# Index stage of a graph network kernel: statistics and roots in pairs of tiles, the running count summed in PSUM

## The chip, the cores and the metric

The kernel runs on one core of a Trainium2 chip. The metric is the device time of one execution in microseconds (us); the median of three runs is compared. TensorE is PE in the rows, VectorE DVE, ScalarE ACT, GpSimd POOL, SyncE SP. "Row sums" below are TensorE's matmuls with a column of ones.

## The reference

A graph block of four residual parts on 10000 nodes of 512 features and 5000 edges: graph convolutions, experts, attention over the edges, and a top-two mixture. Only the start of the first part matters here:

```python
    x = x + _L0_gnn_ref(_layernorm(x, axis=-1), src, dst, ...)
    # in _L0_gnn_ref:
        out_deg = jnp.clip(jax.ops.segment_sum(ones, src, num_segments=N), 1.0)
        in_deg = jnp.clip(jax.ops.segment_sum(ones, dst, num_segments=N), 1.0)
        src_norm = (out_deg ** (-0.5))[:, None]
        dst_norm = (in_deg ** (-0.5))[:, None]
        for i in range(n_layers):
            mu = jnp.mean(x, axis=0)
            var = jnp.var(x, axis=0)
    ...
```

The index stage computes two things at once: for every edge its rank among the edges sorted by source and by target, with both degrees (a counting sort that writes edge records in sorted order to memory), and the sum and the sum of squares of each column of the row-normalized x.

## The kernel before

`index_and_stats` is the first large stage of the program; later stages read what it leaves. The edges stand in 40 columns of 128 (ET = 40), the nodes in 79 tiles of 128 rows (NT = 79; the last has 16 rows). A key is split into a high part (one of NH = 80) and a low part (one of 128); `is_hi` and `is_lo` are its one-hot forms.

Each engine has its own list of instructions, written by hand; semaphores order them. A loop over t, the edge loop, runs through the 40 columns, and two node tiles go along with each turn of it (`reached`). The twelve first tiles (AHEAD) are worked ahead of the loop.

- **Node tiles.** SP loads a tile into a ring of twelve (R). DVE (`stats`, by `layer_norm`) takes the tile's row statistics, aggregates them and adds EPS, three instructions, each waiting for the one before. POOL (`root`) raises the variance to the power -1/2 and forms the shift. ACT (`norm_and_square`) normalizes the tile and squares it. TensorE (`add_up`) adds both up over the rows into psN and psQ, four passes of 512 columns a tile. In turn t, DVE and POOL handle tiles 12+2t and 13+2t, ACT tiles 10+2t and 11+2t, TensorE tiles 8+2t and 9+2t (LAG = 4).
- **Edges.** `seen` is the running count: for each key, where the next edge with it goes. Per turn, TensorE turns the one-hot low parts (`turn`) and counts the column's keys (`histogram`, into psH); DVE adds that count to `seen`; ACT casts `seen` to bf16 (`cast_seen`) and the turned picks (`spread`); DVE forms the rest that the cast lost (`lower`); TensorE looks the counts up from both parts (line 402); DVE takes for each edge its own value out (lines 500 to 510). Every fourth turn DVE writes places and degrees for four columns; POOL then grades them (`grade`, again a power) and scatters two records per column to memory (`scatter`).
- **Order.** In turn t, ACT casts the count of turn t+1 first, then spreads, then normalizes the turn's two tiles. TensorE makes the histogram of turn t+1 at the start of turn t, ahead of the row sums, and looks up after them. POOL's turn is two roots, the grading if it is due, two scatters.

Before the loop, TensorE counts all keys (psL), DVE scans, and TensorE makes the first offsets (lines 385 and 387), which DVE copies to `seen` (line 460).

Of the kernel before, what the change touches and what calls it, by code (L numbers as in the profile page):

```python
# [183 lines left out]
def index_and_stats(nc, g, x, src, dst, attr, total, square):  # L184
# [6 lines left out]
    assert FULL * ET == E and NT <= 2 * ET + AHEAD and ET % G == 0 and 5 * NH <= 512 and EP < 1 << 15  # L191
    with Phase(nc, "index") as ph:
# [9 lines left out]
        seen = ph.sb("seen", [P, 2, 2, NH])  # L202
# [21 lines left out]
        mv = ph.sb("mv", [P, R, 3])  # L224
# [43 lines left out]
        def _(act):  # L268
            def norm_and_square(n):
                r, j, k = node_rows(g, n), n % R, n % S  # L270
                act.wait_ge(rooted, 2 * n + 2)
# [13 lines left out]
            def cast_seen(t):  # L285
                act.wait_ge(counted, t + 1)
# [18 lines left out]
        def _(pool):  # L305
            def root(n):
                r, j = node_rows(g, n), n % R
                pool.wait_ge(stat_step, 3 * n + 3)
                if n >= R:
                    pool.wait_ge(normed, n - R + 1)  # L310
                pool.sem_inc(waited, 1)
                pool.tensor_tensor(rstd[0:r, j:j + 1], mv[0:r, j, 2:3], g.minus_half[0:r, 0:1], ALU.pow).then_inc(rooted, 1)
                pool.wait_ge(rooted, 2 * n + 1)
# [21 lines left out]
            for n in range(AHEAD):  # L335
                root(n)
            for t in range(ET):
                for n in reached(t, 0):
                    root(n)
# [10 lines left out]
        def _(pe):  # L350
# [32 lines left out]
            histogram(0)  # L383
            pe.wait_ge(scanned, 1)
            pe.matmul(psL[:, 1, 0:2 * NH], g.before[:, :], whole[:, :, :].rearrange("l n h -> l (n h)"),
                      start=True, stop=False)
            pe.matmul(psL[:, 1, 0:2 * NH], g.ones[:, :], upto[:, :, :].rearrange("l n h -> l (n h)"),
                      start=False, stop=True).then_inc(based, 1)
# [20 lines left out]
        def _(v):  # L409
            chain = Chain(v, stat_step, 3)  # L410

            def stats(n):
                r, j = node_rows(g, n), n % R
                v.wait_ge(loaded[j], 16 * (n // R + 1))
                if n >= R:
                    v.wait_ge(rooted, 2 * (n - R) + 2)
                chain.at(n)
                layer_norm(v, chain, xt[0:r, j, :], st[:, j, :], mv[:, j, :], r, waited)
                chain.end()
# [15 lines left out]
            for n in range(2):  # L435
# [5 lines left out]
                for stat in range(n * AHEAD // 2, (n + 1) * AHEAD // 2):  # L441
                    stats(stat)
# [17 lines left out]
            v.tensor_copy(seen[:, 0, :, :].rearrange("l n h -> l (n h)"), psL[:, 1, 0:2 * NH]).then_inc(counted, 1)  # L460
            v.wait_ge(counted, 1)
            step(v.tensor_scalar(nodes[:, :, :], seen[:, 0, :, :], -ZERO, None, ALU.add))
# [10 lines left out]
            def lower(t):  # L473
# [3 lines left out]
                v.tensor_tensor(tabs[:, t % 2, 1, 2:5:2, :], seen[:, t % 2, :, :], tabs[:, t % 2, 0, 2:5:2, :],  # L477
# [4 lines left out]
            for t in range(ET):  # L482
                j = t % 2
                if t + 1 < ET:
                    v.wait_ge(histed, t + 1)
                    v.wait_ge(counted, t + 1)
                    if t >= 1:
                        v.wait_ge(lowered, t)
                        v.wait_ge(cast, t)
# [1883 lines left out]
```

## Time and profile before

| | us |
|---|---|
| median of 3 runs | 3903.74 (3902.39 to 3907.45) |
| the profiled execution | 3906.87 |
| its span, first to last instruction | 3905.1 |
| TensorE busy in the span | 3254.1 (83%) |
| DVE busy | 2462.7 (63%) |
| ACT busy | 1388.0 (36%) |
| POOL busy | 1235.2 (32%) |

1.8 us of the profiled execution lie outside its span, and it stands 3.1 us above the median. The shares are means over many stages. The index stage fills the first 280 us of the span, and its edge loop runs from about 56 to 254 us. Busy time counts an operation from its start to its end, so that operations back to back overlap a little. Two ends of one stage are of interest: DVE's last result of the loop, and POOL's last scatter, after which the stage waits for the scattered records to land.

### The profile page before, as it was taken

The numbers are of one execution on the slowest core, as the hardware profiler recorded it, in microseconds if no ns is written. First come the engines' busy times: TensorE is split into PE (matmuls) and PEld (weight loads), VectorE is DVE, ScalarE is ACT, GpSimd is POOL, SyncE is SP. The second block draws the span as 40 slices with busy tenths as digits, with TensorE's granted clock in tenths as the row PEclk, the third lists the DMA queues.
The fourth block names the chain that finished last, engine by engine and source line by source line (L and its number), as shares of the span: only waits on it lengthen the run. The fifth ranks groups of instructions, "written<-read, shape, count | busy, mean of one in ns | idle before, by whom it ended". The sixth has DMA issues, their size and how long they took to land. (4 is left out here: it accounts for less than half of the span.)

```text
span 3905.1 us, 61914 instructions
## 1 busy us (share of the span) xinstructions
PE 3254.1 (83%) x18334; PEld 2750.4 (70%) x18335; DVE 2462.7 (63%) x5844; ACT 1388.0 (36%) x2580; POOL 1235.2 (32%) x1606
## 2 busy tenths in 40 slices
PE   6845889997775309999999999999679992969999
PEld 1213667776774209999999999999668881856766
DVE  7855877644766764545455444454278877957776
ACT  4633655421112314445444444444211111114443
POOL 4752532222551012323222322323123320025552
PEclk9977999997555559999999999999889995989999
DMA  4313323335994034544444444444322111146663
GB/s 157 99 24 105 106 94 122 100 124 167 305 306 135 0 76 113 133 116 136 126 111 137 102 133 143 99 137 113 66 64 59 54 43 42 67 122 149 161 155 104
DMA packets 250361, 449.60 MB, mean 115 GB/s; under 512 B 65632, under 2 KB 71073, under 8 KB 249591
## 3 DMA queue, kind: packets, MB, share of 16 engines
q1 hardware_dynamic: 176425, 280.66, 22.0%
q0 software_dynamic: 62368, 145.38, 17.1%
q10 hardware_dynamic: 11318, 20.54, 1.4%
q8 instruction: 119, 1.95, 0.2%
q14 instruction: 131, 1.07, 0.1%
HBM read 319.38 MB, written 126.83 MB: 114 GB/s over the span
## 5 line engine op out<-in xcount | busy, mean ns | idle before, releaser
L1460 PE MATMUL experts_psU<-experts_x_hi,experts_up_hi 128*128 128x312 f32 (+1 forms) x1408 | 443.3, 315 | 22.9 <-issue 16.5
L1489 PE MATMUL experts_psY<-experts_hid_hi,experts_dn_hi 128*128 128x312 f32 (+1 forms) x1408 | 439.0, 312 | 0.0
L1461 PE MATMUL experts_psU<-experts_x_lo,experts_up_hi 128*128 128x312 f32 (+1 forms) x1408 | 436.8, 310 | 0.0
L1462 PE MATMUL experts_psU<-experts_x_hi,experts_up_lo 128*128 128x312 f32 (+1 forms) x1408 | 435.6, 309 | 0.0
L1490 PE MATMUL experts_psY<-experts_hid_lo,experts_dn_hi 128*128 128x312 f32 (+1 forms) x1408 | 431.3, 306 | 0.0
L1491 PE MATMUL experts_psY<-experts_hid_hi,experts_dn_lo 128*128 128x312 f32 (+1 forms) x1408 | 429.7, 305 | 0.0
L1419 POOL DMA_INDIRECT experts_xg<-xn,experts_token_i x96 | 123.4, 1285 | 663.0 <-DVE experts_token_i L1586 643.5
L1625 DVE TENSOR_TENSOR experts_hid_lo<-experts_hid,experts_hid_hi 128x312 fp32r<-128x312 f32 (+1 forms) x352 | 161.2, 480 | 252.2 <-ACT experts_hid L1552 252.2
L1550 ACT ACTIVATE experts_hid_hi<-experts_psU,experts_bup 128x312 fp32r<-128x312 f32 (+1 forms) x352 | 183.6, 522 | 322.1 <-PE experts_psU L1462 320.3
L1460 PEld LDWEIGHTS experts_psU<-experts_x_hi,experts_up_hi 128*128 128x128 f32 (+1 forms) x1408 | 265.2, 188 | 24.4 <-issue 22.0
L1617 DVE TENSOR_TENSOR experts_dn_lo<-experts_dn_raw,experts_dn_hi 128x1536 fp32r<-128x1536 f32 (+1 forms) x128 | 208.0, 1625 | 98.6 <-ACT experts_dn_hi L1528 98.4
L1461 PEld LDWEIGHTS experts_psU<-experts_x_lo,experts_up_hi 128*128 128x128 f32 (+1 forms) x1408 | 265.6, 189 | 0.0
L1490 PEld LDWEIGHTS experts_psY<-experts_hid_lo,experts_dn_hi 128*128 128x128 f32 (+1 forms) x1408 | 265.5, 189 | 0.0
L1462 PEld LDWEIGHTS experts_psU<-experts_x_hi,experts_up_lo 128*128 128x128 f32 (+1 forms) x1408 | 265.4, 188 | 0.0
L1491 PEld LDWEIGHTS experts_psY<-experts_hid_hi,experts_dn_lo 128*128 128x128 f32 (+1 forms) x1408 | 265.3, 188 | 0.0
L1489 PEld LDWEIGHTS experts_psY<-experts_hid_hi,experts_dn_hi 128*128 128x128 f32 (+1 forms) x1408 | 264.9, 188 | 0.0
L772 PE MATMUL gcn_psZ<-gcn_wa_hi,gcn_agg_hi 128*128 128x512 f32 x480 | 200.8, 418 | 7.5 <-DVE gcn_diff L900 7.5
L1612 DVE TENSOR_TENSOR experts_x_lo<-experts_psT,experts_x_hi 128x416 fp32r<-128x416 f32 x96 | 56.7, 590 | 232.8 <-ACT experts_x_hi L1523 232.8
L1528 ACT CAST experts_dn_hi<-experts_dn_raw 128x1536 fp32r<-128x1536 f32 (+1 forms) x128 | 175.8, 1374 | 57.1 <-PE experts_psY L1491 45.3
L1722 PE MATMUL score_psP<-score_w_hi,score_x_hi 128*128 128x512 f32 x480 | 193.8, 404 | 0.0
L1430 POOL DMA_INDIRECT x<-experts_y,experts_token_i x96 | 157.8, 1644 | 111.6 <-DVE experts_y L1604 84.1
L1723 PE MATMUL score_psP<-score_w_lo,score_x_hi 128*128 128x512 f32 x480 | 190.1, 396 | 0.0
(412 smaller groups left out, 8158.7 us busy)
## 6 DMA issues: line engine op xcount, KB each, us to landing
experts_dn_raw<-in_L_ffn_W_down SPq DMA_DIRECT2D x96, 768.0 KB, 4.6
conv<-gcn_diff SPq DMA_DIRECT2D x120, 256.0 KB, 2.9
experts_up_raw<-in_L_ffn_W_up SPq DMA_DIRECT2D x32, 682.5 KB, 8.4
index_xt<-in_x SPq DMA_DIRECT2D x78, 256.0 KB, 2.8
route_xt<-in_x SPq DMA_DIRECT2D x78, 256.0 KB, 4.9
x<-route_xt SPq DMA_DIRECT2D x78, 256.0 KB, 4.3
xn<-route_xn ACTq DMA_DIRECT2D x78, 256.0 KB, 5.0
two_xt<-x SPq DMA_DIRECT2D x78, 256.0 KB, 2.8
```

Of the source, the lines that this page charges most:

```text
L772: pe.matmul(psZ[:, j % 2, :], agg_hi[:, j, h, :], wa_hi[:, h, :], start=(h == 0), stop=False)
L1460: pe.matmul(acc, up_hi[:, c, cols], x_hi[:, c, :], start=(c == 0), stop=False)
L1461: pe.matmul(acc, up_hi[:, c, cols], x_lo[:, c, :], start=False, stop=False)
L1462: mm = pe.matmul(acc, up_lo[:, c, cols], x_hi[:, c, :], start=False, stop=(c == C - 1))
L1489: pe.matmul(acc, dn_hi[0:w, m, cols], hid_hi[0:w, m, :], start=(m == 0), stop=False)
L1490: pe.matmul(acc, dn_hi[0:w, m, cols], hid_lo[0:w, m, :], start=False, stop=False)
L1491: mm = pe.matmul(acc, dn_lo[0:w, m, cols], hid_hi[0:w, m, :], start=False, stop=(m == M - 1))
L1528: act.copy(dn_hi[:, batch[k][0]:batch[k][-1] + 1, :], dn_raw[:, k % 2, 0:len(batch[k]), :])\
L1550: act.activation(hid_hi[0:width[m], m, :], psU[0:width[m], m % U, 0:K], ACT.Silu, bias=bup[0:width[m], bass.ds(e // GR, 1), m])
L1617: v.tensor_tensor(dn_lo[:, ms, :], dn_raw[:, k % 2, 0:len(batch[k]), :], dn_hi[:, ms, :], ALU.subtract).then_inc(dn_low, 1)
L1722: pe.matmul(acc, hi, w_hi[:, n, c, :], start=(c == 0), stop=False)
L1723: pe.matmul(acc, hi, w_lo[:, n, c, :], start=False, stop=False)
```

## The change

DVE takes the statistics of two tiles (a pair) before it aggregates either, adds EPS to both in one instruction, and forms the negated means in another (`mv` gets a fourth column). POOL takes the power of two tiles in one instruction and forms both shifts with one product. The last, single tile makes a pair of one.

The running count `seen` is no longer added up by DVE. It lives in psH: `histogram(t)` now makes the count of turn t+1 out of four matmuls into one bank, the cast part of the count of turn t through the identity, the two one-hot counts of column t, and the rest part through the identity. ACT's cast and DVE's `lower` read psH. The first offsets go to psH too.

```diff
+                if t == 0:
+                    act.wait_ge(counted, 1)
+                else:
+                    act.wait_ge(histed, t)
-                act.copy(tabs[:, t % 2, 0, 2:5:2, :], seen[:, t % 2, :, :]).then_inc(cast, 1)
+                act.copy(tabs[:, t % 2, 0, 2:5:2, :], psH[:, t % 2, 0:2 * NH].rearrange("l (n h) -> l n h", n=2)).then_inc(cast, 1)
...
-            def root(n):
+            def root(p):
+                n, w = 2 * p, min(2, NT - 2 * p)
...
-                pool.tensor_tensor(rstd[0:r, j:j + 1], mv[0:r, j, 2:3], g.minus_half[0:r, 0:1], ALU.pow).then_inc(rooted, 1)
+                pool.tensor_tensor(rstd[0:r, j:j + w], mv[0:r, j:j + w, 2], g.minus_half[0:r, 0:w], ALU.pow).then_inc(rooted, 1)
...
-                pool.tensor_scalar(shift[0:r, j:j + 1], mv[0:r, j, 0:1], -1.0, rstd[0:r, j:j + 1],
-                                   ALU.mult, ALU.mult).then_inc(rooted, 1)
+                pool.tensor_tensor(shift[0:r, j:j + w], mv[0:r, j:j + w, 3], rstd[0:r, j:j + w], ALU.mult).then_inc(rooted, 1)
...
             def histogram(t):
-                if t >= 2:
-                    pe.wait_ge(counted, t)
+                to = psH[:, (t + 1) % 2, :]
+                pe.matmul(to[:, 0:2 * NH], identb[:, :], tabs[:, t % 2, 0, 2:5:2, :], start=True, stop=False)
                 for n in range(2):
-                    mm = pe.matmul(psH[:, t % 2, n * NH:(n + 1) * NH], is_lo[:, n, t, :], is_hi[:, n, t, :],
-                                   start=True, stop=True)
-                mm.then_inc(histed, 1)
+                    pe.matmul(to[:, n * NH:(n + 1) * NH], is_lo[:, n, t, :], is_hi[:, n, t, :], start=False, stop=False)
+                pe.matmul(to[:, 0:2 * NH], identb[:, :], tabs[:, t % 2, 1, 2:5:2, :], start=False, stop=True)                    .then_inc(histed, 1)
...
                 if t + 1 < ET:
                     turn(t + 1)
-                    histogram(t + 1)
                 for stat in reached(t, LAG):
                     add_up(stat)
                 pe.wait_ge(picked, t + 1)
                 pe.wait_ge(lowered, t + 1)
+                if t + 1 < ET:
+                    histogram(t)
...
+                for k in range(w):
+                    v.wait_ge(loaded[j + k], 16 * (n // R + 1))
+                    v.sem_inc(waited, 1)
+                    chain.go(v.bn_stats(st[0:r, j + k, :], xt[0:r, j + k, :]))
+                for k in range(w):
+                    chain.wait(6 * p + 1 + k)
+                    v.sem_inc(waited, 1)
+                    chain.go(v.bn_aggr(mv[0:r, j + k, 0:2], st[0:r, j + k, :]))
+                chain.wait(6 * p + 2 * w)
+                chain.go(v.tensor_scalar(mv[0:r, j:j + w, 2], mv[0:r, j:j + w, 1], EPS, None, ALU.add))
+                chain.go(v.tensor_scalar(mv[0:r, j:j + w, 3], mv[0:r, j:j + w, 0], -1.0, None, ALU.mult))
...
-                    v.tensor_tensor(seen[:, (t + 1) % 2, :, :], seen[:, t % 2, :, :],
-                                    psH[:, t % 2, 0:2 * NH].rearrange("l (n h) -> l n h", n=2), ALU.add).then_inc(counted, 1)
-                for stat in reached(t, 0):
+                for stat in reached(t, 0)[::2]:
                     stats(stat)
```

TensorE's instructions in one turn of the edge loop before; L354 and L356 are the row sums of two tiles, L402 the look-up, L363 the turning, L370 the histogram:

```order
L354 MATMUL index_psN<-index_xn,all_ones 1x512 [waits index_normed]
L356 MATMUL index_psQ<-index_xsq,all_ones 1x512 [waits index_squared]
...
L402 MATMUL index_psL<-index_tabs,index_pick 128x240 [waits index_look_step,index_lowered,index_picked]
L402 MATMUL index_psL<-index_tabs,index_pick 128x240
L402 MATMUL index_psL<-index_tabs,index_pick 128x160 x2
L363 MATMUL index_psT<-index_identb,index_is_lo 128x128 [waits index_picked]
L363 MATMUL index_psT<-index_identb,index_is_lo 128x128
L370 MATMUL index_psH<-index_is_hi,index_is_lo 128x80 [waits index_counted]
```

The same turn on TensorE with the change (L371 to L374 the new histogram, L404 the look-up, L366 the turning):

```order
L357 MATMUL index_psN<-index_xn,all_ones 1x512 [waits index_normed]
L359 MATMUL index_psQ<-index_xsq,all_ones 1x512 [waits index_squared]
...
L371 MATMUL index_psH<-index_tabs,index_identb 128x160 [waits index_lowered,index_picked]
L373 MATMUL index_psH<-index_is_hi,index_is_lo 128x80 x2
L374 MATMUL index_psH<-index_tabs,index_identb 128x160
L404 MATMUL index_psL<-index_tabs,index_pick 128x240 [waits index_look_step]
L404 MATMUL index_psL<-index_tabs,index_pick 128x240
L404 MATMUL index_psL<-index_tabs,index_pick 128x160 x2
L366 MATMUL index_psT<-index_identb,index_is_lo 128x128 [waits index_picked]
```

The histogram has moved from behind the look-up, a turn ahead, to between the row sums and the look-up, and has two matmuls more.

ACT's instructions in one turn before; L289 is the cast of the count, L283 the spread, L274 and L277 the normalization and the square:

```order
L289 CAST index_tabs<-index_seen 128x2x80 [waits index_looked,index_counted]
L283 CAST index_pick<-index_psT 128x256 [waits index_looked,index_turned]
L274 ACTIVATE index_xn<-index_xt,index_shift,index_rstd 128x512 [waits index_summed,index_rooted]
L277 ACTIVATE index_xsq<-index_xn 128x512 [waits index_normed]
L274 ACTIVATE index_xn<-index_xt,index_shift,index_rstd 128x512 [waits index_summed,index_rooted]
```

And ACT's turn with the change:

```order
L292 CAST index_tabs<-index_psH 128x2x80 [waits index_looked,index_histed]
L283 CAST index_pick<-index_psT 128x256 [waits index_looked,index_turned]
L274 ACTIVATE index_xn<-index_xt,index_shift,index_rstd 128x512 [waits index_summed,index_rooted]
L277 ACTIVATE index_xsq<-index_xn 128x512 [waits index_normed]
L274 ACTIVATE index_xn<-index_xt,index_shift,index_rstd 128x512 [waits index_summed,index_rooted]
```

The order is the same; the cast waits for TensorE's histogram (`histed`) where it waited for DVE's addition (`counted`).

## Rows read from the trace of the kernel before

**Rows 1.** Busy table, one stretch: us, then busy engines, granted clock, DMA

```profile
140.00:160.00 20.00, 15.65 (x58) 4.11 (x58) 18.03 (x62) 13.29 (x24) 15.43 (x24) 1.00 0.35 95
```

**Rows 2.** POOL's timeline: start us, us, engine, line, operation [idle before <-releaser]

```profile
103.08 1.66 POOL L322 TENSOR_TENSOR index_norm<-index_deg,all_minus_half 128x8 f32<-128x8 f32 x1
...
105.59 1.06 POOL L332 DMA_INDIRECT recS<-index_recS,index_place  x1 [0.47 <-POOL index_recD L326]
...
107.95 0.58 POOL L312 TENSOR_TENSOR index_rstd<-index_mv,all_minus_half 128x1 f32<-128x1 f32 x1
...
110.38 1.06 POOL L332 DMA_INDIRECT recS<-index_recS,index_place  x1 [0.39 <-issue]
...
124.28 1.66 POOL L322 TENSOR_TENSOR index_norm<-index_deg,all_minus_half 128x8 f32<-128x8 f32 x1
```

**Rows 3.** Timeline of DVE, one turn of the edge loop

```profile
123.85 0.31 DVE L490 TENSOR_TENSOR index_seen<-index_seen,index_psH 128x160 f32<-128x160 f32 x1
...
124.08 0.69 DVE L134 BATCH_NORM_STATS2 index_st<-index_xt 128x6 f32<-128x512 f32 x1
...
124.90 0.18 DVE L136 BATCH_NORM_AGGREGATE index_mv<-index_st 128x2 f32<-128x6 f32 x1
...
126.56 0.32 DVE L477 TENSOR_TENSOR index_tabs<-index_seen,index_tabs 128x160 bf16<-128x160 f32 x1
...
128.71 0.31 DVE L490 TENSOR_TENSOR index_seen<-index_seen,index_psH 128x160 f32<-128x160 f32 x1
```

**Rows 4.** Timeline of ACT and TensorE (PE), the same turn

```profile
124.19 0.33 ACT L289 CAST index_tabs<-index_seen 128x160 bf16<-128x160 f32 x1 [1.56 <-DVE index_seen L490]
...
124.69 0.81 ACT L274 ACTIVATE index_xn<-index_xt,index_shift,index_rstd 128x512 f32<-128x512 f32 x1
...
125.56 1.02 PE L354 MATMUL index_psN<-index_xn,all_ones 128*1 128x512 f32 x2 [0.67 <-ACT index_xn L274]
...
129.08 0.52 PE L402 MATMUL index_psL<-index_tabs,index_pick 128*128 128x240 bf16 x4
...
129.55 0.23 PE L370 MATMUL index_psH<-index_is_hi,index_is_lo 128*128 128x80 bf16 x2
```

**Rows 5.** Groups by line and shape, 0 to 330 us: busy, mean ns

```profile
L402 PE MATMUL index_psL<-index_tabs,index_pick 128*128 128x160 bf16 x80 | 12.9, 246 | 0.0
...
L370 PE MATMUL index_psH<-index_is_hi,index_is_lo 128*128 128x80 bf16 x80 | 9.7, 205 | 4.9 <-DVE index_seen L490 4.9
```

**Rows 6.** Timeline of TensorE and DVE after a long pause

```profile
195.65 1.62 PE L354 MATMUL index_psN<-index_xn,all_ones 128*1 128x512 f32 x2 [2.82 <-ACT index_xn L274]
...
200.87 0.52 PE L402 MATMUL index_psL<-index_tabs,index_pick 128*128 128x240 bf16 x4
...
201.43 0.41 DVE L505 TENSOR_TENSOR index_prod<-index_psL,index_is_hi 128x240 f32<-128x240 f32 x1 [1.41 <-PE index_psL L402]
```

**Rows 7.** Busy table in stretches of 1 us, columns as in rows 1

```profile
172.00:173.00 1.00, 0.00 (x0) 0.00 (x0) 0.81 (x3) 0.00 (x0) 0.78 (x2) 1.00 0.03 2
...
197.00:198.00 1.00, 1.00 (x3) 0.21 (x2) 0.78 (x4) 1.00 (x3) 0.69 (x2) 0.50 0.58 181
```

**Rows 8.** Timeline at the start of the edge loop

```profile
49.89 0.43 PE L387 MATMUL index_psL<-index_upto,all_ones 128*128 128x160 f32 x2
...
51.20 0.32 DVE L460 COPY index_seen<-index_psL 128x160 f32<-128x160 f32 x1
...
56.93 0.33 ACT L289 CAST index_tabs<-index_seen 128x160 bf16<-128x160 f32 x1 [4.78 <-DVE index_seen L490]
```

**Rows 9.** Timeline at the end of the index stage

```profile
239.03 0.31 ACT L289 CAST index_tabs<-index_seen 128x160 bf16<-128x160 f32 x1
...
243.10 0.17 DVE L520 CAST index_recD<-index_look 128x4 int32<-128x4 f32 x1
...
245.47 1.68 POOL L322 TENSOR_TENSOR index_norm<-index_deg,all_minus_half 128x8 f32<-128x8 f32 x1
...
269.67 0.95 POOL L332 DMA_INDIRECT recD<-index_recD,index_place  x1 [0.31 <-issue]
```

More of the change, by code:

```diff
@@ L190, in index_and_stats @@
     R, S, G, AHEAD, LAG = 12, 6, 4, 12, 4
-    assert FULL * ET == E and NT <= 2 * ET + AHEAD and ET % G == 0 and 5 * NH <= 512 and EP < 1 << 15
+    assert AHEAD % 2 == R % 2 == 0 and NT % 2 == 1 and FULL * ET == E and NT <= 2 * ET + AHEAD and ET % G == 0 and 5 * NH <= 512 and EP < 1 << 15
     with Phase(nc, "index") as ph:
@@ L201, in index_and_stats @@
         identb = ph.sb("identb", [P, P], BF16)
-        seen = ph.sb("seen", [P, 2, 2, NH])
+        seen = ph.sb("seen", [P, 2, NH])
         whole = ph.sb("whole", [P, 2, NH])
@@ L223, in index_and_stats @@
         st = ph.sb("st", [P, R, 6])
-        mv = ph.sb("mv", [P, R, 3])
+        mv = ph.sb("mv", [P, R, 4])
         rstd = ph.sb("rstd", [P, R])
@@ L270, in norm_and_square @@
                 r, j, k = node_rows(g, n), n % R, n % S
-                act.wait_ge(rooted, 2 * n + 2)
+                act.wait_ge(rooted, n // 2 * 2 + 2)
                 if n >= S:
@@ L333, in scatter @@
                                             rec[:, t, :], None).then_inc(scattered, 16)
-            for n in range(AHEAD):
-                root(n)
+            for p in range(AHEAD // 2):
+                root(p)
             for t in range(ET):
-                for n in reached(t, 0):
-                    root(n)
+                for n in reached(t, 0)[::2]:
+                    root(n // 2)
                 if t >= G:
@@ L382, in _ @@
             turn(0)
-            histogram(0)
             pe.wait_ge(scanned, 1)
-            pe.matmul(psL[:, 1, 0:2 * NH], g.before[:, :], whole[:, :, :].rearrange("l n h -> l (n h)"),
+            pe.matmul(psH[:, 0, 0:2 * NH], g.before[:, :], whole[:, :, :].rearrange("l n h -> l (n h)"),
                       start=True, stop=False)
-            pe.matmul(psL[:, 1, 0:2 * NH], g.ones[:, :], upto[:, :, :].rearrange("l n h -> l (n h)"),
+            pe.matmul(psH[:, 0, 0:2 * NH], g.ones[:, :], upto[:, :, :].rearrange("l n h -> l (n h)"),
                       start=False, stop=True).then_inc(based, 1)
@@ L409, in _ @@
         def _(v):
-            chain = Chain(v, stat_step, 3)
+            chain = Chain(v, stat_step)
             def stats(n):
+                p, w = n // 2, min(2, NT - n)
                 r, j = node_rows(g, n), n % R
-                v.wait_ge(loaded[j], 16 * (n // R + 1))
                 if n >= R:
[L416 to L419, printed above, removed]
+                    v.wait_ge(rooted, n - R + 2)
+                for k in range(w):
[9 more added lines that the diff above has]
+                chain.go(v.tensor_scalar(mv[0:r, j:j + w, 3], mv[0:r, j:j + w, 0], -1.0, None, ALU.mult))
             v.memset(keys[:, :, :], PAD).then_inc(padded, 1)
@@ L440, in _ @@
                 v.sem_inc(hot, 1)
-                for stat in range(n * AHEAD // 2, (n + 1) * AHEAD // 2):
+                for stat in range(n * AHEAD // 2, (n + 1) * AHEAD // 2, 2):
                     stats(stat)
@@ L459, in _ @@
             v.wait_ge(based, 1)
-            v.tensor_copy(seen[:, 0, :, :].rearrange("l n h -> l (n h)"), psL[:, 1, 0:2 * NH]).then_inc(counted, 1)
+            v.tensor_copy(seen[:, :, :].rearrange("l n h -> l (n h)"), psH[:, 0, 0:2 * NH]).then_inc(counted, 1)
             v.wait_ge(counted, 1)
-            step(v.tensor_scalar(nodes[:, :, :], seen[:, 0, :, :], -ZERO, None, ALU.add))
+            step(v.tensor_scalar(nodes[:, :, :], seen[:, :, :], -ZERO, None, ALU.add))
             step(v.scalar_tensor_tensor(nodes[:, :, :], whole[:, :, :], 0.0, nodes[:, :, :], ALU.is_gt, ALU.mult))
@@ L476, in lower @@
                     v.wait_ge(looked, t - 1)
-                v.tensor_tensor(tabs[:, t % 2, 1, 2:5:2, :], seen[:, t % 2, :, :], tabs[:, t % 2, 0, 2:5:2, :],
+                v.tensor_tensor(tabs[:, t % 2, 1, 2:5:2, :], psH[:, t % 2, 0:2 * NH].rearrange("l (n h) -> l n h", n=2),
+                                tabs[:, t % 2, 0, 2:5:2, :],
                                 ALU.subtract).then_inc(lowered, 1)
@@ L483, in _ @@
                 j = t % 2
[L484 to L489, printed above, removed]
-                    v.tensor_tensor(seen[:, (t + 1) % 2, :, :], seen[:, t % 2, :, :],
-                                    psH[:, t % 2, 0:2 * NH].rearrange("l (n h) -> l n h", n=2), ALU.add).then_inc(counted, 1)
-                for stat in reached(t, 0):
+                for stat in reached(t, 0)[::2]:
                     stats(stat)
```

7 lines of the change are left out of this document (3 added, 4 removed).

## The prediction

> **What bounds the kernel now.** The page's chain of waits covers only the end of the program, so I read the index stage from its own views, in this order: the busy table by stage, then one engine's timeline after the other, always asking whether a row waits for another engine or only for its own work.
>
> The busy table calls VectorE (DVE) the fullest engine of the stage, 18.03 us of 20, with GpSimd (POOL) at 15.43 and TensorE at 15.65, at full granted clock [rows 1]. POOL's timeline says otherwise: the idle time before its rows is its own issue and its own results, 0.4 to 0.5 us, so POOL is not waiting for anyone [rows 2]. One round of four turns of the edge loop lasts 124.28 - 103.08 = 21.20 us, 5.30 us a turn: grading 2.51 (103.08 to 105.59), each pair of scatters 2.36 (105.59 to 107.95), each two roots 2.43 (107.95 to 110.38). DVE is close behind: one turn lasts 128.71 - 123.85 = 4.86 us [rows 3], and every fourth has four short operations more (in [rows 9] the last of them starts at 243.10, the next turn waits for it). So the stage's pace is 5.30 us a turn, set by POOL with DVE just under it, and POOL alone works from the end of the turns to the end of the stage at 270.62 [rows 9].
>
> **The change part by part.**
>
> *DVE.* Two statistics last 126.56 - 124.08 = 2.48 us a turn now; the first stands 0.82 before its aggregation although it works 0.69, the rest is waiting for its own result [rows 3]. Of one tile's 1.24 us, 0.42 are left for the aggregation and the short operation. In a pair the second statistic fills the first one's wait: 0.69 + 0.82 + 0.42 + about 0.1 for one short operation more = 2.0 us (estimate; 1.8 if the short ones overlap too, 2.48 if nothing is gained). The running-count addition goes: 124.08 - 123.85 = 0.23. DVE's turn falls from 4.86 to about 4.15.
>
> *POOL.* 8 columns of the power take 1.66 us, one takes 0.58 [rows 2], so each further column is about 0.15 and a pair 0.73; with its product and two waits some 1.2 us instead of 2.43. POOL's turn falls from 5.30 to about 4.1. Both old limits are lifted by more than a microsecond, over some 34 turns.
>
> *TensorE and ScalarE (ACT).* TensorE gets two more matmuls of 160 columns a turn: 800 columns in four matmuls take 0.52 us, 160 columns in two 0.23 [rows 4]. The new group has four matmuls and 480 columns; on the line between those two it takes 0.38 us (low end 0.23, high end 0.52). In work this would fit: row sums 3.52 (below), 0.70 from the look-up to the old histogram's end (129.55 + 0.23 - 129.08), and about 0.2 more make 4.4 us a turn.
>
> What decides is where the new group stands. Before, the count of turn t+1 was a DVE addition, and its histogram had been made one turn earlier, ahead of the row sums. Now `histogram(t)` is the count itself, it stands behind the row sums of turn t, and ACT's cast of the count for turn t+1 waits for it. Behind that cast on ACT's queue stand the transposed picks and the two normalizations of the turn, and TensorE's row sums of turn t+1 are exactly the sums of these two tiles (tiles 10+2t and 11+2t: ACT's list runs two tiles behind AHEAD, TensorE's LAG = 4 behind, one turn apart). So a closed circle appears: histogram(t), cast, spread, normalization, two tiles' row sums, histogram(t+1). No engine can run ahead in it. Its length, from rows:
> - cast to the first row sum: 125.56 - 124.19 = 1.37 us [rows 4];
> - first row sum to whatever follows the second tile: 129.08 - 125.56 = 3.52 us [rows 4];
> - the new group: 0.38 us, and 0.04 from a matmul's end to its reader (200.87 + 0.52 = 201.39, reader at 201.43) [rows 6].
> Sum: 5.31 us, against 5.30 now. The relief of POOL and DVE turns into waiting. The low end of the group gives 5.16, the high end 5.45; that the cast now reads PSUM moves its 0.33 by a few hundredths at most, since the cast of the picks reads PSUM already. DVE keeps slack: its turn takes about 4.15, with grading about a microsecond more, and what it forms after a cast TensorE needs only a turn later.
>
> A regular pause stays in TensorE: it stands idle 0.67 us before the turn's first row sum [rows 4], at full clock over the 20 us around it [rows 1]. The Trainium skill, page "TensorE: Matmul & The Clock Gate", section "A second HAM failure mode: psum-queue depth-cycling", says that short idle times between groups of matmuls that change PSUM banks in every iteration can make the clock swing. The trace so far speaks against it for pauses of this size; by the trace the turn stays at 5.31; by that rule the loop would pay for falls of the clock, 3915.8 as rival B works it out.
>
> *Ends.* Start: the count's base now reaches DVE when TensorE has made it, at 49.89 + 0.43 + 0.04 = 50.36, not at 51.20, when DVE had come to it [rows 8]: DVE's three late pairs save it 1.4 us. The early pairs save up to 0.5 more, one pair's gain, as far as the loads allow; I take 0.27. The first cast of the loop then comes 0.84 + 0.27 earlier, less about 0.2 since the group (0.42) is longer than the addition that stood there: 56.93 becomes 56.0. End: 34 circles later, 56.0 + 34 x 5.31 = 236.5; the last one has a single tile, 1.37 + 1.76 + 0.42 = 3.6: the cast of turn 36 at 240.1, now 239.03 [rows 9]. From it to the last result that the ninth grading needs it is 243.10 + 0.17 - 239.03 = 4.24 us now, at most as much afterwards; without a wait on the way it is 0.34 for the cast, 128.71 - 126.56 = 2.15 from `lower` to the turn's end [rows 3], and about 1.0 for the four short operations, 3.5. So 243.6 to 244.3. POOL, today still busy with older scatters, starts that grading at 245.47; freed, it starts at 243.6 to 244.3. From there to POOL's end it works 25.15 us without a pause in either kernel [rows 9].
>
> The sum: 1.1 to 1.9 us earlier, I take 1.5. Nothing behind the stage changes. The profiled execution (3906.87) would become 3905.4; its median of runs is 3903.74, so **3902.2 us**. A measurement of this kernel tells about 0.2% (7.8 us) from no change.
>
> **The rivals.**
>
> A: *the relief counts.* If the circle did not close (row sums free to lag), the longest engine would set the turn: TensorE or DVE at about 4.4 us (DVE 4.15 and a quarter of its long turn's extra). 34 x (5.31 - 4.41) = 31 us more: 3872. For it: both old limits do fall. Against: the order of ACT's and TensorE's instructions, which leaves TensorE no tile that it could add up ahead.
>
> B: *the clock falls inside the circle.* After a pause of 2.82 us the four row sums of a turn took 200.87 - 195.65 = 5.22 instead of 3.52 [rows 6], at granted 0.50, the level of 1.2 GHz [rows 7]; a pause that fills the microsecond from 172 passed at 1.00 [rows 7]. Each such fall costs 1.70 us; today POOL's pace hides it, in the circle nothing does. With one fall in every round of four turns, as often as DVE's long turns come, 8 falls: 3902.2 + 13.6 = 3915.8, slower. It is slower by over 0.2% from six falls on. Against it: DVE's long turn no longer stops TensorE, so the long pauses of today should vanish and only the regular one remain.
>
> C: *the group does not overlap.* If each of its matmuls waited for the one before, it would take 0.246 + 2 x 0.205 + 0.246 = 0.90 us [rows 5], 0.52 more in each of 34 turns: 3902.2 + 17.7 = 3919.9, slower; it decides from 0.28 us more a turn on. Against: the same kind of chain, four matmuls into one bank in pairs, takes 0.52 for more columns [rows 4].
>
> **How the numbers follow.** Forecast 0.79, A 0.04, B 0.09, C 0.08. The forecast's own range: the group's ends give 34 x -0.15 = -5.1 and 34 x +0.14 = +4.8, the start 0.3 either way, and up to three falls of the clock, as many as I count in the loop today (one of them is shown), +5.1: 3896 to 3912. That leaves out the rivals, 0.21, so the range need not reach further. Faster by over 0.2% (under 3895.9): A and a remnant of the forecast, 0.06. Slower (over 3911.5): B and C, 0.16 with a little taken off for cases short of the bound. Same: 0.78.
>
> **What would show it.** Right: DVE's additions gone and its statistics in pairs of about 2.0 us; POOL's power rows of about 0.73 us that now wait for DVE; ACT's casts released by TensorE's new matmuls, 5.3 us apart in every turn, with no long turn at the fourth; TensorE's only pause in a turn that of about 0.7 us before the first row sum; the stage's last scatter one or two microseconds earlier. Wrong: casts about 4.4 us apart (A); stretches at granted 0.50 between 60 and 230 us with casts 7 us apart (B); the new group longer than 0.65 us (C); or a normalization that waits for POOL.

## The result and the profile after

| | before | after |
|---|---|---|
| median of six runs, us | 3904.84 (3901.09 to 3907.45) | 3921.82 (3918.70 to 3926.89) |
| ratio, 95% interval | | 1.0045 (1.0032 to 1.0058) |
| the profiled execution | 3906.87 | 3918.70 |
| its span | 3905.1 | 3917.0 |

The changed kernel is slower by 17.0 us between the medians, 0.45% by the ratio. The forecast was 3902.2, its range ended at 3912.

I look at the index stage first, since it alone was changed. The busy table, over the stretch of [rows 1] and over the whole loop (us, then busy PE, PEld, DVE, ACT, POOL, granted clock, DMA share, GB/s):

```profile
140.00:160.00 20.00, 16.35 (x71) 4.74 (x70) 15.71 (x57) 12.40 (x24) 13.20 (x18) 1.00 0.36 98
60.00:240.00 180.00, 149.00 (x620) 42.40 (x619) 136.31 (x500) 108.87 (x203) 108.48 (x145) 1.00 0.30 83
```

DVE fell from 18.03 to 15.71 of 20 us, POOL from 15.43 to 13.20, and the clock is whole over the loop. One turn in the timeline of after, all engines (start, us, engine, line, operation, idle time before and what ended it); it answers [rows 3] and [rows 4]:

```profile
120.05 0.23 PE L374 MATMUL index_psH<-index_tabs,index_identb 128*128 128x160 bf16 x1
...
120.32 0.29 ACT L292 CAST index_tabs<-index_psH 128x160 bf16<-128x160 f32 x1 [1.97 <-PE index_psH L374]
...
120.99 0.91 POOL L316 TENSOR_TENSOR index_rstd<-index_mv,all_minus_half 128x2 f32<-128x2 f32 x1 [2.79 <-DVE index_mv L429]
...
121.65 1.02 PE L357 MATMUL index_psN<-index_xn,all_ones 128*1 128x512 f32 x2 [0.91 <-ACT index_xn L274]
...
122.83 1.27 DVE L422 BATCH_NORM_STATS2 index_st<-index_xt 128x6 f32<-128x512 f32 x2
...
124.03 0.41 DVE L426 BATCH_NORM_AGGREGATE index_mv<-index_st 128x2 f32<-128x6 f32 x2
...
124.55 0.16 DVE L429 TENSOR_SCALAR index_mv<-index_mv 128x2 f32<-128x2 f32 x1
...
125.18 0.24 PE L371 MATMUL index_psH<-index_tabs,index_identb 128*128 128x160 bf16 x1
...
125.33 0.23 PE L374 MATMUL index_psH<-index_tabs,index_identb 128*128 128x160 bf16 x1
...
125.60 0.29 ACT L292 CAST index_tabs<-index_psH 128x160 bf16<-128x160 f32 x1 [1.97 <-PE index_psH L374]
```

Read from the cast at 120.32 to the next at 125.60 it is the circle of the prediction, step by step: cast to first row sum 1.33, row sums to the new group 3.53, group 0.38 (125.18 to 125.56), 0.04 to the cast. From the cast at 62.27 to that at 236.43 every turn is 5.28. POOL now waits 2.79 us for DVE; nobody waits for POOL. At the end of the stage, in the same columns, the answer to [rows 9]:

```profile
236.43 0.29 ACT L292 CAST index_tabs<-index_psH 128x160 bf16<-128x160 f32 x1 [1.97 <-PE index_psH L374]
...
239.97 0.29 ACT L292 CAST index_tabs<-index_psH 128x160 bf16<-128x160 f32 x1 [1.62 <-PE index_psH L374]
...
243.59 1.67 POOL L325 TENSOR_TENSOR index_norm<-index_deg,all_minus_half 128x8 f32<-128x8 f32 x1 [2.23 <-DVEq L524]
...
267.55 0.96 POOL L335 DMA_INDIRECT recD<-index_recD,index_place  x1 [0.30 <-issue]
```

The last scatter starts 2.1 us earlier than before (267.55 against 269.67). So the stage that was changed behaved as forecast, and the loss lies behind it. Taking the first and last start of the instructions on one tile of each later stage, one stage stands out: **the experts**, whose code the change does not touch. From the first weight load for `experts_psU` to ACT's last reading of it, it is 2775.7 - 1467.2 = 1308.5 us before and 2784.6 - 1459.6 = 1325.0 after, 16.5 us more. The spans differ by 11.9, so the other stages together are 4.6 us shorter in this pair of executions, 2.1 of it from the index stage; I come back to the rest.

TensorE does the experts in a hardware loop (`tiles`, lines 97 and 1502 of the kernel before): five rounds of four experts, with four branches back to the loop's head. The groups of instructions by line, before and then after (busy us, mean ns of one, idle time before them and what ended most of it; "issue" is idle time for which the profile shows no cause):

```profile
L1460 PE MATMUL experts_psU<-experts_x_hi,experts_up_hi 128*128 128x312 f32 (+1 forms) x1408 | 443.3, 315 | 22.9 <-issue 16.5 <-DVE experts_x_lo L1612 4.2 <-ACT experts_hid L1552 2.2
L1461 PE MATMUL experts_psU<-experts_x_lo,experts_up_hi 128*128 128x312 f32 (+1 forms) x1408 | 436.8, 310 | 0.0
```

```profile
L1463 PE MATMUL experts_psU<-experts_x_hi,experts_up_hi 128*128 128x312 f32 (+1 forms) x1408 | 444.2, 315 | 21.8 <-issue 15.8 <-DVE experts_x_lo L1615 4.4 <-ACT experts_hid L1555 1.6
L1464 PE MATMUL experts_psU<-experts_x_lo,experts_up_hi 128*128 128x312 f32 (+1 forms) x1408 | 437.4, 311 | 13.6 <-issue 13.6
```

The first of the three matmul lines had 16.5 us of unexplained idle time before, and has 15.8 now. The second line had none, and has 13.6 us. Where they lie is seen in TensorE's timeline around the first branch back, before and then after:

```profile
1918.43 0.30 PE L1491 MATMUL experts_psY<-experts_hid_hi,experts_dn_lo 85*128 85x312 f32 x1
1922.90 0.49 PE L1460 MATMUL experts_psU<-experts_x_hi,experts_up_hi 128*128 128x312 f32 x1 [4.17 <-issue]
1923.19 0.46 PE L1461 MATMUL experts_psU<-experts_x_lo,experts_up_hi 128*128 128x312 f32 x1
```

```profile
1908.91 0.30 PE L1494 MATMUL experts_psY<-experts_hid_hi,experts_dn_lo 85*128 85x312 f32 x1
1912.94 0.62 PE L1463 MATMUL experts_psU<-experts_x_hi,experts_up_hi 128*128 128x312 f32 x1 [3.72 <-issue]
...
1914.66 0.46 PE L1463 MATMUL experts_psU<-experts_x_hi,experts_up_hi 128*128 128x312 f32 x1
1918.61 0.42 PE L1464 MATMUL experts_psU<-experts_x_lo,experts_up_hi 128*128 128x312 f32 x1 [3.48 <-issue]
```

Before, TensorE stops once behind each branch, for about 4 us. After, it stops, does seven matmuls, and stops again for 3.5 us: four times 3.4 is the 13.6. The rest of the 16.5 is the clock: from the 8th matmul behind a branch to the 41st it takes about 1 us longer after than before. The busy table of TensorE for the 50 us of the first and second branch (columns: us, busy, granted clock, DMA), before and then after:

```profile
1900.00:1950.00 50.00, 45.83 (x315) 0.97 0.50 148
2050.00:2100.00 50.00, 46.01 (x309) 0.93 0.60 180
```

```profile
1900.00:1950.00 50.00, 42.80 (x284) 0.90 0.47 145
2050.00:2100.00 50.00, 42.56 (x278) 0.86 0.53 158
```

Behind such an idle time TensorE runs at the 1.2 GHz level (a matmul every 0.26 us instead of 0.14) before the higher one comes back, and with two idle times it stays there longer.

### The profile page after: what moved, and what is told of

The parts are those of the page before. It is cut to its first block and busy times, and to the rows that moved or that the text cites. A ratio compares the mean times of both kernels' runs of the same rounds, so it can differ in the third digit from the quotient of the medians.

```text
span 3917.0 us, 61795 instructions
## 1 busy us (share of the span) xinstructions
PE 3263.4 (83%) x18410; PEld 2758.9 (70%) x18411; DVE 2440.4 (62%) x5806; ACT 1383.7 (35%) x2580; POOL 1200.1 (31%) x1528
## 5 line engine op out<-in xcount | busy, mean ns | idle before, releaser
L1463 PE MATMUL experts_psU<-experts_x_hi,experts_up_hi 128*128 128x312 f32 (+1 forms) x1408 | 444.2, 315 | 21.8 <-issue 15.8
L1464 PE MATMUL experts_psU<-experts_x_lo,experts_up_hi 128*128 128x312 f32 (+1 forms) x1408 | 437.4, 311 | 13.6 <-issue 13.6
L1465 PEld LDWEIGHTS experts_psU<-experts_x_hi,experts_up_lo 128*128 128x128 f32 (+1 forms) x1408 | 265.9, 189 | 14.2 <-issue 14.2
```

The source lines that it names most:

```text
L1463: pe.matmul(acc, up_hi[:, c, cols], x_hi[:, c, :], start=(c == 0), stop=False)
L1464: pe.matmul(acc, up_hi[:, c, cols], x_lo[:, c, :], start=False, stop=False)
L1465: mm = pe.matmul(acc, up_lo[:, c, cols], x_hi[:, c, :], start=False, stop=(c == C - 1))
```

## The experiments

**Theory T1.** The change lengthens TensorE's list of instructions ahead of the experts loop: four matmuls for the count of each of 39 columns instead of two for each of 40, 156 - 80 = 76 more. A matmul is two instructions, its weight load and itself (the profile counts 18334 matmuls and 18335 weight loads before, 18410 and 18411 after). So everything behind stands 152 instructions later: ahead of the first matmul into `experts_psU` the traces record 9897 instructions of TensorE before and 10049 after. If TensorE's instructions come in pieces of fixed size, the loop's head now stands elsewhere in its piece: close to the end, so that soon after each branch back TensorE has to wait for the next piece as well. **Rival T2:** something in the changed work (other data, other timing of DMA) slows the experts.

The Trainium skill, page "Runtime: NRT & Kernel Launch", section "Instruction fetch mechanics", describes such pieces: 256 instructions each, fetched in sequence, a buffer of 2048 on TensorE, and a fetch that has to be waited for when a taken branch leads out of what is held. The traces agree on the size, with one packet of instructions for each 254 executed (below). From one branch back to the next they record 2423 instructions, more than those 2048; no run here measured the buffer itself. This page of the Trainium skill gives no time for the wait.

T1 can be tested by other lengths of the list alone.

**e1_before_76: only the length.**

```diff
             for stat in range(AHEAD + 2 * ET - LAG, NT):
                 add_up(stat)
+            for more in range(76):
+                pe.matmul(psT[:, 0, 0:P], is_lo[:, 0, more % ET, :], identb[:, :], start=True, stop=True)
```

> The kernel before, with 76 small matmuls more on TensorE behind its last row sum of the index stage, where it then only waits for the stage's end; their result is never read. 76 is the number by which the change lengthens TensorE's program ahead of the experts loop. Theory T1 (place of the code): the changed kernel lost its time in the experts loop, whose code is the same, because the loop's head moved against the pieces in which TensorE's instructions are fetched. It expects the second idle time of about 3.5 us behind each of the loop's four branches here too, eight instead of four rows of idle time put down to issue (30 us in all, not 16.5), the experts stage 14 to 17 us longer, the index stage unchanged, and 3917 to 3923 us. Rival T2 (the counts or the pairs themselves: other data in SBUF and PSUM, earlier start of later stages, other DMA timing) expects the time of the kernel before, 3901 to 3908, and four rows of idle time.

Measured: 3923.80 us (ratio to before 1.0047, 1.0030 to 1.0063), and the experts take 1326.4 us, 17.9 more than before; both lie just above what was expected. The groups by line show the second idle time:

```profile
L1463 PE MATMUL experts_psU<-experts_x_lo,experts_up_hi 128*128 128x312 f32 (+1 forms) x1408 | 436.8, 310 | 14.2 <-issue 14.2
```

The weight load and the matmul that enclose it, from the timeline of PEld and of PE behind the first branch:

```profile
1921.19 0.33 PEld L1463 LDWEIGHTS experts_psU<-experts_x_lo,experts_up_hi 128*128 128x128 f32 x1
...
1925.28 0.42 PE L1463 MATMUL experts_psU<-experts_x_lo,experts_up_hi 128*128 128x312 f32 x1 [3.63 <-issue]
```

So the loss comes back without any of the change, from 76 matmuls whose result nobody reads. T2 falls.

**e2_after_52: the length made up to 256.** The same two lines with 52, in the changed kernel.

> The changed kernel with 52 such matmuls at the same place: with the 76 of the change TensorE's program ahead of the experts loop is then longer than before by 128 matmuls, 256 instructions. T1, if the pieces are of 256 instructions, expects the loop's head at the same place of a piece as before: the second idle time behind the branches gone, the experts stage back to about 1307 us, and 3900 to 3906 us, the gain of the index stage (2 us) and of the route stage (6 us, if that isn't chance) kept: 3897 to 3905. T2 expects 3918 to 3925, as the changed kernel. A wrong size of the piece would leave the second idle time there, perhaps at another matmul.

Measured: 3902.16 us (ratio 0.9992, 0.9982 to 1.0001); experts 1306.2 us; no idle time on the second line:

```profile
L1466 PE MATMUL experts_psU<-experts_x_lo,experts_up_hi 128*128 128x312 f32 (+1 forms) x1408 | 435.4, 309 | 0.0
```

With 256 instructions more than before, the loop's head is back where it was in its piece, and the loss is gone. What is left between the medians is 2.1 us, which is what the index stage should give, but the interval does not tell it from nothing.

**e3_pairs and e4_count: the halves of the change.** e3 has the pairs of DVE and POOL and the running count of before; e4 the count on TensorE and the statistics of before. The core of e3, against the changed kernel:

```diff
-                pe.matmul(to[:, 0:2 * NH], identb[:, :], tabs[:, t % 2, 0, 2:5:2, :], start=True, stop=False)
+                if t >= 2:
+                    pe.wait_ge(counted, t)
...
+                    v.tensor_tensor(seen[:, (t + 1) % 2, :, :], seen[:, t % 2, :, :],
+                                    psH[:, t % 2, 0:2 * NH].rearrange("l (n h) -> l n h", n=2), ALU.add).then_inc(counted, 1)
```

> The pairs of tiles alone: statistics on VectorE and roots on GpSimd as in the changed kernel, the running count as in the kernel before (an addition on VectorE). TensorE's program is word for word that of the kernel before. T1 expects the experts stage as before, with four idle times behind branches. For the index stage the circle of the prediction (count on TensorE, cast, normalizations, row sums, 5.3 us) is not there: VectorE's turn would be 4.86 - 0.6 = about 4.25 and a quarter microsecond for the grading, GpSimd's about 4.1, TensorE's about 4.1, so about 4.5 us a turn instead of 5.30, over some 32 turns 26 us: about 3879 us (3872 to 3890). If the stage had another limit of 5.3 us a turn that the prediction overlooked, the time would stay at 3900 to 3906.

The core of e4, against the changed kernel:

```diff
-                for k in range(w):
-                    v.wait_ge(loaded[j + k], 16 * (n // R + 1))
...
+                chain.at(n)
+                layer_norm(v, chain, xt[0:r, j, :], st[:, j, :], mv[:, j, :], r, waited)
+                chain.end()
```

> The running count on TensorE alone: statistics and roots tile by tile as in the kernel before. TensorE's program is that of the changed kernel. T1 expects the second idle times in the experts loop: 14 to 17 us there. In the index stage GpSimd's 5.30 us a turn and the circle's 5.28 stand side by side, so it stays within 3 us of before. Sum: 3916 to 3924 us. T2, if the pairs were the cause, expects about 3904; if the count is the cause, about 3920 as well, so this run tells only which half of the change does it.

Measured: e3 3873.58 us (0.9919, 0.9902 to 0.9936), experts 1307.3 us; e4 3926.51 us (1.0057, 1.0040 to 1.0074; 2.5 us over the expected range), experts 1325.9 us. The half that lengthens TensorE's list has the loss, the other hasn't. And e3 says more: without the count on TensorE, the index stage is far shorter, its last scatter at 241.97. ACT's casts of the count in e3, four turns (one round):

```profile
111.34 0.32 ACT L289 CAST index_tabs<-index_seen 128x160 bf16<-128x160 f32 x1 [2.03 <-issue]
...
129.29 0.33 ACT L289 CAST index_tabs<-index_seen 128x160 bf16<-128x160 f32 x1 [2.04 <-DVE index_seen L498]
```

17.95 us, 4.49 a turn instead of 5.28, and DVE sets it: in this round no operation of DVE waits for another engine, and it is busy 18.97 of 20 us in the stretch of [rows 1]:

```profile
140.00:160.00 20.00, 18.50 (x69) 4.96 (x69) 18.97 (x73) 14.71 (x27) 15.11 (x20) 1.00 0.44 122
```

**e5_lag6 and e9_hist_first: the circle opened.** The theory C1 of the prediction is that a closed circle holds the changed stage at 5.28 us. Its rival C2 is that the count on TensorE costs that much by itself. e5 lets the row sums run one turn later; e9 puts the new group ahead of them. Both have the 52 matmuls of e2.

```diff
-    R, S, G, AHEAD, LAG = 12, 6, 4, 12, 4
+    R, S, G, AHEAD, LAG = 12, 6, 4, 12, 6
```

```diff
-                for stat in reached(t, LAG):
-                    add_up(stat)
-                pe.wait_ge(picked, t + 1)
                 pe.wait_ge(lowered, t + 1)
                 if t + 1 < ET:
                     histogram(t)
+                for stat in reached(t, LAG):
+                    add_up(stat)
+                pe.wait_ge(picked, t + 1)
```

> The changed kernel with LAG 6 instead of 4 (TensorE sums the rows of a tile one turn later), and with the 52 matmuls that put the experts loop's head back. Theory C1 (the closed circle holds the index stage at 5.28 us a turn): with a turn between normalization and row sums the circle is open, the turn falls to what VectorE or TensorE need, 4.2 to 4.5 us, and the last scatter comes 24 to 32 us earlier than in the changed kernel: 3869 to 3880 us. Rival C2 (the count on TensorE costs the relief by itself, by the group's own time or by casts that read PSUM): the turn stays at 5.2 to 5.3 us, 3898 to 3904 us.

> The changed kernel with the group that forms the count put ahead of the turn's row sums instead of behind them, LAG 4 as it is, and with the 52 matmuls. C1 expects the circle open here too, since the cast no longer stands behind the row sums: 4.2 to 4.6 us a turn, 3869 to 3884 us. C2 expects 5.2 to 5.3 us a turn and 3898 to 3904 us. If the wait for the lower part of the count, which now stands ahead of the row sums, becomes the new limit, the turn is between the two.

Measured: e5 3870.96 us (0.9915, 0.9898 to 0.9931), e9 3875.57 us (0.9936, 0.9920 to 0.9953). Casts of e5 over one round, and its busy table:

```profile
113.36 0.29 ACT L292 CAST index_tabs<-index_psH 128x160 bf16<-128x160 f32 x1 [0.98 <-PE index_psH L374]
...
130.54 0.29 ACT L292 CAST index_tabs<-index_psH 128x160 bf16<-128x160 f32 x1 [0.61 <-PE index_psH L374]
```

```profile
140.00:160.00 20.00, 20.00 (x80) 5.40 (x77) 17.98 (x68) 14.47 (x27) 14.92 (x21) 1.00 0.44 122
```

17.18 us for four turns, 4.30 each, with TensorE now without a pause: it sets the pace. The last scatter starts at 239.68. In e9 it is 242.66, with turns of 3.9 us and one of 5.9 in each round. C2 falls: the same group of four matmuls, read by the same casts from PSUM, stands in both. Only its place in the circle made the 5.28. Both kernels, and e3, beat the kernel before and the changed one: the pairs alone gain 30.7 us (e3), and the count on TensorE, placed as in the change, takes nearly all of that back by closing the circle.

**How the loop's place costs time: e6, e8, e10, e7.** All four are the kernel before with a longer list, in the place of e1: 84, 88 and 68 matmuls, and in e8 152 semaphore increments instead of 76 matmuls:

```diff
+            for more in range(152):
+                pe.sem_inc(idle, 1)
```

> The kernel before with 84 small matmuls in the idle time at the end of the index stage, eight more than in the run with 76. By the place of the second idle time (behind 2 commands and 7 matmuls, 16 instructions, of the loop) T1 puts the end of a piece 16 instructions behind the loop's head there; 8 matmuls more put the head at the beginning of a piece. T1 expects no second idle time, four rows of idle time put down to issue, the experts stage at 1306 to 1310 us and 3901 to 3908 us, so less than with 76. A rival in which additional work or a longer program as such costs the time expects 3918 us or more.

> The kernel before with 152 semaphore increments on TensorE's queue at the place of the 76 matmuls: as many instructions (a matmul is two, its weight load and itself), but no work of TensorE and no data. T1 expects the second idle time in the experts loop at the same matmul, the stage 14 to 18 us longer and 3917 to 3925 us. Were it the matmuls (their work, the clock, PSUM), it would be 3901 to 3908 us.

Measured: e8 3923.39 us (1.0052, 1.0035 to 1.0068), 13.7 us of second idle times. Neither the matmuls' work nor their data matter, the number of instructions does. But e6 was a miss: 3925.31 us (1.0057, 1.0041 to 1.0074), experts 1328.5. Its timeline at the first branch has one idle time, as expected, but of twice the length, and all four sum to 38.2 us:

```profile
1914.99 0.30 PE L1493 MATMUL experts_psY<-experts_hid_hi,experts_dn_lo 85*128 85x312 f32 x1
1924.73 0.62 PE L1462 MATMUL experts_psU<-experts_x_hi,experts_up_hi 128*128 128x312 f32 x1 [9.43 <-issue]
```

I had counted wrong by one. In e1 the weight load at 1921.19 (above) stands ahead of the second idle time and its matmul behind it: two commands, eight weight loads and seven matmuls, 17 instructions, lie ahead of the end of the piece, not 16. Sixteen instructions more leave one in the old piece, and TensorE waits for two pieces before it can do anything. The trace of e6 records it: behind the first branch TensorE's first command stands at 1918.86, the second only at 1924.64, and 5.5 to 5.7 us lie between the two behind all four branches. The next two runs were set by this reading.

> The kernel before with 88 small matmuls in the idle time at the end of the index stage. With 84 the loop had one idle time of 9.4 us behind each branch, ahead of its first matmul, as long as both idle times and the seven matmuls between them with 76. Read by T1: the end of a piece lay one instruction behind the head, so that two pieces had to come before any work. Four matmuls more put the head 7 instructions into the next piece, which holds 249 of the loop's instructions. T1 expects one idle time of 4 us behind each branch, 16 to 17 us in all, the experts stage at 1306 to 1310 us and 3900 to 3908 us. Rival T3 (a program longer by some 70 matmuls or more costs this time wherever its pieces end) expects 3918 to 3928 us.

> The kernel before with 68 such matmuls: by T1 the end of a piece lies 33 instructions behind the head, behind 15 matmuls instead of 7. In the runs with 76 and 152 the second piece was there 5.4 to 5.7 us after the loop's first matmul. If it is asked for together with the first or as soon as that has come, 15 matmuls of 0.26 us (3.9 us) hide part of it: idle time of 1.3 to 1.9 us ahead of the 16th matmul, four times, the experts stage at 1313 to 1319 us and 3908 to 3915 us. If it is asked for only when the first is used up, the idle time there is 3.4 to 3.8 us as before, the stage 1322 to 1328 us and 3917 to 3925 us.

Measured: e10 3906.11 us (1.0009, 0.9999 to 1.0019), experts 1306.8 us, no second idle time. Adding four matmuls to e6 takes 19 us away; a longer list costs nothing by itself. e7 lies between: 3913.22 us (1.0028, 1.0017 to 1.0038), experts 1313.6 us. Its first branch:

```profile
1919.46 0.41 PE L1462 MATMUL experts_psU<-experts_x_hi,experts_up_hi 128*128 128x312 f32 x1 [4.01 <-issue]
...
1924.99 0.31 PE L1462 MATMUL experts_psU<-experts_x_hi,experts_up_hi 128*128 128x312 f32 x1 [1.67 <-issue]
```

The second idle time now comes ahead of the 16th matmul. It lasts 1.67 here and 1.27, 1.25 and 1.00 behind the other branches, 1.3 on average, at the low end of the 1.3 to 1.9 expected. From the first matmul to the first one out of the next piece it is 5.53 us in e7, 5.39 in e1 and 5.67 in the changed kernel at the first branch: the second piece comes at its own time, and what the first one holds is work that hides the wait.

**The pieces are on record.** Each profile's table of DMA queues (packets, MB, share of 16 engines) has a queue of the kind "instruction" whose packets follow TensorE's list. The kernel before, e2 and e1:

```profile
q8 instruction: 119, 1.95, 0.2%
```

```profile
q8 instruction: 120, 1.97, 0.2%
```

```profile
q8 instruction: 124, 2.03, 0.2%
```

Every packet is of 16,384 bytes. While TensorE works through 6362 instructions of the kernel before (1483.2 to 1920.2 us), 25 of them start, one for 254 instructions. e2, with 256 instructions more than before, has one packet more; e1 has five more, one for its longer list and one for each of four rounds of the loop, which take twelve packets instead of eleven. Behind each branch of the experts loop, in all twelve kernels, the first packet starts 3.6 to 4.4 us and the second 9.3 to 10.7 us after the branch, wherever the head lies: the second piece is asked for at about the same time, whether TensorE already stands waiting for it or not. And only this loop pays for it: its branches back are recorded with 6.0 to 6.7 us, those of the program's other TensorE loops, whose bodies have at most 936 instructions, with 0.2 us.

All kernels of this comparison in one table (instructions between the head and the end of its piece: 17 counted in e1 and the rest from the lengths of the lists; the kernel before, run again beside the others, had medians of 3904.28, 3903.19 and 3902.84):

| kernel | instructions left | idle "issue" behind the branches, us | experts, us | median, us |
|---|---|---|---|---|
| before | 169 | 16.5 | 1308.5 | 3904.84 |
| e10 (+88 matmuls) | 249 | 16.6 | 1306.8 | 3906.11 |
| e2 (after, +52) | 169 | 16.0 | 1306.2 | 3902.16 |
| e7 (+68) | 33 | 21.1 | 1313.6 | 3913.22 |
| e1 (+76) | 17 | 15.9 + 14.2 | 1326.4 | 3923.80 |
| e8 (+152 increments) | 17 | 16.0 + 13.7 | 1325.5 | 3923.39 |
| after | 17 | 15.8 + 13.6 | 1325.0 | 3921.82 |
| e6 (+84) | 1 | 38.2 | 1328.5 | 3925.31 |

## Why the prediction was wrong

**Right: the circle.** Its sum was 5.31 us, it measured 5.28: 1.33 for 1.37, 3.53 for 3.52, 0.38 and 0.04 as forecast. TensorE's pause ahead of the first row sum is 0.91, not about 0.7. That it was the circle that ate the relief, and not some cost of the count, is shown by e5 and e9, where the relief appears as soon as it is open.

**Right: the relief of DVE and POOL.** The pair was put at 2.0 us; in the shown turn it lasts 122.83 to 124.71, 1.88. POOL's power of a pair took 0.91 us and not the 0.73 drawn from one column and eight, which cost nothing since POOL waits. Rival A priced an open circle at 3872 with turns of about 4.41; e5 has 4.30 and 3870.96, with TensorE as the limit, one of the two that A named. A did not happen here because the order closes the circle, the argument given against it.

**Right: the ends.** The first cast was put at 56.0 and came at 56.28; one fall of the clock behind it made the first turn 5.99. The cast of turn 36 was put at 240.1 (239.97), the ninth grading at 243.6 to 244.3 (243.59), the gain at 1.1 to 1.9 (2.1, just above). In the kernels e1, e6, e7, e8 and e10, whose index stage up to the added instructions is that of before, the last scatter starts at 271.2 to 272.4, so 269.67 was an early one and the gain may be larger than 2.1. The forecast of the whole was 3902.2, and with the loop's place restored (e2) the kernel takes 3902.16; that the two agree to a tenth is luck, since the interval of e2 is some 4 us wide to either side.

**Wrong: one sentence.** "Nothing behind the stage changes." The change by parts counted the new matmuls' time in the stage, and gave the stages behind it a zero because their code is the same. Their place in TensorE's list is not. That term was 16.5 us in the profiled pair, and no rival held it. The runs add up: e1, with the longer list alone, lost 19.5 us, and 19.5 less the index stage's 2.1 is close to the 17.0 measured. The rows that could have warned were in the trace of before: 16.5 us of idle time at four branches, on the engine that bounds the experts, put down to no cause. I had read only the index stage's rows.

**Right number, wrong cause: rivals B and C.** B gave 3915.8 and C 3919.9, and the result lies near them. Neither happened: the granted clock of the index stage is 1.00 from 60 to 240 us in spite of the 0.91 us pause in every turn, and the group takes 0.38 us, not 0.90.

**Left open.** In the profiled pair the route stage is 6.2 us shorter after (from its first transpose into `route_psT` to the last copy out of it, 260.5 us against 266.7), and the last stage 2.7 us longer (412.0 against 409.3, from its first transpose to the last reading of `two_psO`). With DVE's and GpSimd's lists as before, e1, e7 and e10 have 263.1, 262.5 and 260.3 in the route stage. So executions scatter by some microseconds in that stage, or the place of TensorE's code matters a little there as well; single profiles don't tell these apart. That the spans of the profiled pair differ by 11.9 us and the medians by 17.0 is such scatter too: the profiled execution lies 2.0 us above its median before and 3.1 below it after.

## What to carry to other kernels

An edit that adds instructions to an engine moves all that stands behind them on that engine. Where a later stage is a hardware loop whose branch back has to wait for its instructions (here one of 2423 instructions did, those of up to 936 did not), its time depends on where its head lies: look for idle time without a cause behind the branches, and run the old kernel with as many idle instructions added, before the edit itself is blamed or praised. And when two engines are relieved by handing their chain to a third, follow the chain around once: if it comes back to its start within one turn, the relief only turns into waiting, until a lag or another order opens it.

## What the runs showed of the hardware

- A branch back in a loop of 2423 instructions costs TensorE 3.7 to 4.4 us of idle time each time, in every kernel here but e6, where it is 9.4 to 9.6, and some matmuls at the 1.2 GHz level behind it. The branch itself is recorded with 6.0 to 6.7 us; in the loops of at most 936 instructions with 0.2 us.
- The next piece of instructions comes 5.4 to 5.7 us after the first work out of the piece with the loop's head at the first branch of e1, e7 and the changed kernel, and 5.2 to 6.4 over the 20 branches of the five kernels with two idle times. Fewer than some 20 matmuls of 0.26 us in between (estimate from 5.5 / 0.26) leave part of that as idle time, up to 9.6 us a branch for both pieces if the head is the last instruction of its piece (e6). In a loop of four branches this moved the time of the kernel by up to 0.57%.
- The pieces are of 256 instructions: one packet of 16,384 bytes starts for every 254 instructions counted in a long stretch, 256 more restored the time (e2), and the loop's head crossed a border between 84 and 88 added matmuls (e6, e10). The Trainium skill, page "Runtime: NRT & Kernel Launch", section "Instruction fetch mechanics", gives this size too.
